# Where ScalarE copies two accumulated tiles within its step of a biased attention

## What is computed

```python
Q, K, V = (proj(Wq, bq), proj(Wk, bk), proj(Wv, bv))
scores = jnp.einsum('bhqd,bhkd->bhqk', Q, K) / math.sqrt(D_K)
scores = scores + _rel_bias_matrix(rel_bias, S)[None]
attn = jax.nn.softmax(scores, axis=-1)
out = jnp.einsum('bhqk,bhkd->bhqd', attn, V)
out = out.transpose(0, 2, 1, 3).reshape(B, S, D_MODEL)
return out @ Wo.T + bo
```

## Time and profile before

| | |
|---|---|
| median of the runs shown | 1761.59 us |
| the profiled execution | 1765.84 us |
| its span, first to last instruction | 1763.7 us |
| busy share of the span, PE / DVE / ACT / POOL | 87% / 76% / 69% / 62% |
| `bias_attention` in it | about 596 to 983 us |

### The profile page before, as it was taken

One profiled execution on the slowest core, in us unless ns is written; L12 is line 12 of the kernel. 1 busy time (PEld: TensorE's weight loads), 2 busy tenths in 40 slices (PEclk: granted clock), 3 DMA queues, 4 the chain that ended last, 5 costly groups with the idle time before them and its releaser, 6 DMA issues. The chain is left out here.

```text
span 1763.7 us, 44299 instructions
## 1 busy us (share of the span) xinstructions
PE 1527.7 (87%) x16988; PEld 1174.0 (67%) x16988; DVE 1331.8 (76%) x2187; ACT 1215.3 (69%) x2065; POOL 1099.1 (62%) x661
## 2 busy tenths in 40 slices
PE   5899996999999498888988569899988999999985
PEld 4577774666666266666666457777777777777774
DVE  5899974545555599999999488888888888888753
ACT  2677774444444477777777358788888888888863
POOL 1667652444445377787777467676677767777614
PEclk8899998999999699999999679999999999999997
DMA  5000000000000500000000001111111111111113
GB/s 169 2 3 3 3 3 15 15 8 7 7 7 1 179 2 2 13 2 14 2 13 2 21 16 29 26 26 26 26 26 26 25 26 26 26 26 26 26 26 102
DMA packets 56839, 44.14 MB, mean 25 GB/s; under 512 B 28152, under 2 KB 47900, under 8 KB 56388
## 3 DMA queue, kind: packets, MB, share of 16 engines
q1 hardware_dynamic: 56644, 41.45, 8.8%
HBM read 17.75 MB, written 4.23 MB: 12 GB/s over the span
## 5 line engine op out<-in xcount | busy, mean ns | idle before, releaser
L832 POOL TENSOR_TENSOR a_prob<-a_prob,a_top 128x1024 f32<-128x1024 f32 x128 | 239.7, 1893 | 66.4 <-DVE a_top L1023 66.3
L1235 POOL TENSOR_TENSOR e_hh<-e_h,e_hh 128x512 fp32r<-128x512 f32 x112 | 144.0, 1289 | 162.2 <-ACT e_hh L1219 160.7
L1494 POOL TENSOR_TENSOR i_qk<-i_qk,i_rt 128x1024 f32<-128x1024 f32 x64 | 152.0, 2375 | 46.5 <-DVE i_rt L1937 41.9
L1504 POOL TENSOR_TENSOR i_qk<-i_qk,i_rn 128x1024 f32<-128x1024 f32 x64 | 122.5, 1914 | 83.1 <-DVE i_rn L1916 83.1
L978 ACT ACTIVATE a_probT<-ps 128x1024 f32<-128x1024 f32 x128 | 131.5, 1027 | 54.3 <-PE ps L908 54.3
L1256 DVE TENSOR_TENSOR e_h<-ps,e_sg 128x512 f32<-128x512 f32 x112 | 77.3, 690 | 119.1 <-PE ps L1118 89.8
L1793 ACT ACTIVATE i_prob<-i_prob,i_top 128x128 f32<-128x128 f32 x512 | 156.4, 392 | 15.3 <-DVE i_top L1925 13.4
L1202 ACT ACTIVATE e_sg<-ps 128x512 f32<-128x512 f32 x112 | 67.0, 598 | 136.3 <-PE ps L1118 136.3
L1020 DVE TENSOR_TENSOR a_prob<-ps,a_table 128x1024 f32<-128x1024 f32 x128 | 150.4, 1216 | 12.1 <-PE ps L900 8.5
L1491 POOL TENSOR_TENSOR i_qk<-i_raw,i_rot 128x1024 f32<-128x1024 f32 x59 | 140.1, 2374 | 24.6 <-issue 24.6
L1023 DVE TENSOR_REDUCE a_top<-a_prob 128x4 f32<-128x1024 f32 x128 | 150.1, 1215 | 6.2 <-issue 0.4
(11 more groups left out here) (305 smaller groups left out, 4375.4 us busy)
## 6 DMA issues: line engine op xcount, KB each, us to landing
i_V<-i_V SPq DMA_DIRECT2D x96, 130.0 KB, 2.3
a_table<-skew_scratch SPq DMA_DIRECT2D x2, 2048.0 KB, 12.3
X<-in_L_attn_x SPq DMA_DIRECT2D x4, 512.0 KB, 6.1
a_table<-in_c_l_table SPq DMA_DIRECT2D x1, 2048.0 KB, 8.1
e_xs<-Y SPq DMA_DIRECT2D x8, 256.0 KB, 2.3
i_ms<-Y SPq DMA_DIRECT2D x16, 128.0 KB, 2.4
i_ms<-Y SPq DMA_DIRECT2D x16, 112.0 KB, 2.4
out_dram<-X SPq DMA_DIRECT2D x7, 256.0 KB, 2.3
```

The source lines that it names most:

```text
L832: nc.gpsimd.tensor_tensor(s, s, top[:, slot].unsqueeze(2).broadcast_to([P, HG, KW]), ALU.subtract).then_inc(shifted, 1)
L1235: nc.gpsimd.tensor_tensor(hh[0:n, b % HBUF, 1, :], h[0:n, b % HBUF, :], hh[0:n, b % HBUF, 0, :].bitcast(F32), ALU.subtract).then_inc(h_lo, 1)
L1494: nc.gpsimd.tensor_tensor(s, s, rt[:], ALU.add).then_inc(rotated, 1)
L1504: nc.gpsimd.tensor_tensor(flat, flat, rn[:, T // TPB % 2, T % TPB].unsqueeze(2).broadcast_to([P, 2 * FH, FD]), ALU.mult).then_inc(qk_done, 1)
```

## The change

ACT's `keep_sums` moves from behind the jobs and `exp` to the head of its step. Nothing else changes.

```diff
             for step in range(FIRST, LAST):
+                T, at = divmod(step - 1, NU)
+                if at == 0 and 1 <= T <= TILES:
+                    keep_sums(T - 1)
                 for n, kind, i, tile in jobs_at(step, 0):
                     job(n, kind, i, tile)
                 if 0 <= step + 1 < UNITS:
                     exp(step + 1)
-                T, at = divmod(step - 1, NU)
-                if at == 0 and 1 <= T <= TILES:
-                    keep_sums(T - 1)
                 if 0 <= step < UNITS:
                     keep_probT(step)
```

## The result

The changed kernel takes 1747.28 us (median of 10 runs, 1745.72 to 1758.61); the kernel before, measured again beside it, 1765.15 us (10 runs, the three of the median above among them, 1760.49 to 1771.67). The ratio is 0.9915, 95% interval 0.9894 to 0.9936: about 15 us faster (11 to 19); the two medians alone lie 17.9 us apart. The profiled execution of the changed kernel is the longest of its ten (1758.61 us). Ahead of the attention stage, where the code is the same, it comes 7.4 us later to its first `x` than the kernel before did, and its granted clock there was in part lower (0.97 to 0.98 between 300 and 500 us against 1.00); what else made it long is not shown. The attention stage can be compared by its own time.

A forecast was written before the change was run, and what follows sets the result against it. The prediction took a loop through PE and ACT as the bound, PE waiting before `d` for ACT's copy. 14 x 1.05 = 14.7 us plus 0.5 made 15.2 us, off the median 1761.59: 1746.4 us, range 1740 to 1752.

The forecast's parts named there:

- The copy costs nothing: ACT's 0.38 us copy, moved to the step's head, fits ACT's idle time: cost 0, bounds 0 and 1.1 us.
- In the qk tile the gain ends at `y`: `d` can start 1.21 us earlier, but `y` then waits for POOL's `oT`: gain 0.0, bounds 0.0 and 1.13 us.
- In the v tile the gain stays, 1.05 us of a possible 1.07: `d` starts 1.07 us earlier and `oT` comes nearly soon enough: `y` gains 1.05 us, bounds 0.74 and 1.07.
- the sum: Whole stage: 14 v tiles at 1.05 us, 0.5 in the last, qk and last three tiles 0; 15.2 us.
- DVE helps the v tile by 0.31 us: DVE, no longer late from the qk tile, starts the v tile's bias sum 0.31 us earlier, bringing `oT` forward.
- The rival by which POOL holds the v tile back: POOL's maxima come no sooner, so the v tile gains only 0.74 us: 1750.8 us; chance 0.13.
- DVE has 21.80 us of work a pair and does not bind: DVE needs 10.90 us a tile, 21.80 for two, below the 22.17 us the loop is to take.
- The first rival: DVE becomes the bound and the qk tile gains too: 21.3 us faster, 1740.3 us; chance 0.12.
- The last v tile gains 0.5 us instead of 1.05, the ends nothing: The stage's end follows DVE and POOL: 0.5 us, between 0.31 and 1.05; the last three tiles 0.
- The mask has 0.6 us to spare: POOL's masking of the keys, behind two subtractions, keeps 0.6 us of its 1.16 us slack.
- the rival that ended slower: Lengthened DVE work makes POOL's subtractions, hence the mask and `y`, late: 1770.6 us at 2.3 us late; chance 0.03.

## Why the prediction was right

- *The copy costs nothing.* Right: it runs in the idle time ahead of the projection's copy, of which 0.65 us are left in the qk tile. The projection's copy still waits for PE.
- *In the qk tile the gain ends at `y`.* Right, and shown by two runs: alone it gives 0, and with `oT` sooner the wait is gone. From the copied keys to `y` it took 807.43 - 800.40 = 7.03 us and takes 806.45 - 799.46 = 6.99: 0.04 less, the difference between 807.43 and the 807.39 at which the prediction had `oT` ready. The profile counts the wait of 0.93 us from the modelled end of the transposes. Counted as the prediction did, 0.93 us behind their start at 804.43, PE could have begun at 805.36, 1.09 us sooner than it did, where 1.1 were worked out.
- *In the v tile the gain stays, 1.05 us of a possible 1.07.* Right: counted from the copied keys, `y` came at 818.57 - 800.40 = 18.17 us and comes at 816.61 - 799.46 = 17.15, 1.02 sooner. But POOL is now the last to arrive here too. The profile puts this `y` down to ACT's copy of the `x` tokens, which ended at 816.44; `oT` ended at 816.46, and `y` begins 0.15 us behind the end of `oT` in both tiles (806.30 to 806.45, 816.46 to 816.61). The pair lost 1.14 us. The other 0.12 came behind this `y`, where the transposes wait for ACT's copy of the ones before, and the sum had nothing for that.
- *DVE helps the v tile by 0.31 us.* Right: counted from the copied keys, `oT` ended at 817.69 - 800.40 = 17.29 us and ends at 816.46 - 799.46 = 17.00, 0.29 sooner; and without the qk tiles' early copy the pair is 0.25 us longer. The rival by which POOL holds the v tile back, with a gain of 0.74 us, is answered by the same rows.
- *DVE has 21.80 us of work a pair and does not bind.* Right: 21.69 when it binds. The first rival's 21.3 us came only when POOL's order was changed as well (15.6 + 5.5 = 21.1 us of stage time). The Trainium skill, page Perfetto Trace Analysis, section Identifying the Most-Contended Engine, has the engine with the highest occupancy optimised first, with weight loads (and the share of peak FLOPs, which the prediction left aside) in place of matmul time for TensorE. In this trace that pointed to DVE (290.94 of 320 us), which was the next bound and not this one; that the pair would shrink to DVE's time at once was the prediction's own reading of it.
- *The last v tile gains 0.5 us instead of 1.05, the ends nothing.* Right for the tile: from its reciprocal to the last one of the stage it took 980.49 - 953.84 = 26.65 us and takes 971.90 - 945.74 = 26.16, 0.49 less. The ends lost 0.9 us in the profiled execution, as shown above.
- *The mask has 0.6 us to spare.* It waits 0.56 us for the keys, so the rival that ended slower was never near.

The sum was 0.4 us short of the stage's own 15.6, and 1746.4 us stands beside 1747.28. That nearness is partly luck. The 14 pairs gave 16.0 us (16.5 between the first and the last reciprocal, less 0.49 behind the last v tile's), where 14.7 were put down, and the ends, at their lower clock, took 0.9 back. The kernel before measured 1765.15 us over ten runs, 3.6 us more than the median from which the 15.2 us were taken.

## What to carry to other kernels

When a wait is taken off the busiest engine, follow that engine to its next wait before counting the gain, and work out when what it needs there is ready, even if the profile shows no idle time in front of it: zero idle time can mean that two chains arrive together. An engine that is off the critical path sets that second time by the order written for it, and moving one instruction in that order can be worth a good part of the change itself: here 5.5 us of stage time, beside the 15.6 of the change.

## What the runs showed of the hardware

Waits of PE of 1.36 and 0.97 us in each pair (kernel before) or of 0.93 us (changed kernel) left the granted clock at 1.00 (2.4 GHz). One of 3.15 us in each pair (`oT` later in the qk tiles) was followed by about 6 us at 0.50 (1.2 GHz), and that cost 2.98 us a pair, more than the added wait itself (2.22 us). A stall on PE is not priced by its length alone.
